# Three kinds of moves at the head of a routed expert stage: first two jobs, segments' and gates' products, register loads, fills

## The reference

```python
h = mod(x_flat[:, :2].sum(axis=1).astype(int32), 8)      # x_flat: layer-normed x
sel = stack([h, mod(h + 1, 8)], axis=1)                  # two neighbouring experts for a token
for e in range(8):
    w = any(sel == e, axis=1) / 2
    out += w[:, None] * (relu(x_flat @ W1[e] + b1[e]) @ W2[e] + b2[e])
x = x + tanh(g_ffn[1]) * out
```

## Time and profile before

| | us |
|---|---|
| median of 3 runs | 358.47 (357.48 to 359.72) |
| the profiled execution | 358.9 |
| its span in the trace | 357.1 |
| TensorE busy | 306.1 (86%) |
| VectorE busy | 195.1 (55%) |
| ScalarE busy | 158.2 (44%) |
| GpSimd busy | 163.3 (46%) |

### The profile page before, as it was taken

The page is one execution under the profiler, slowest core; times in us unless marked ns, Lnnn a source line. Parts: engine busy times, 40 slices in busy tenths (PEclk is TensorE's granted clock), DMA queues, the critical chain, the costliest instruction groups (busy, mean ns, idle before and its releaser), DMA issues.

```text
span 357.1 us, 8461 instructions
## 1 busy us (share of the span) xinstructions
PE 306.1 (86%) x2870; PEld 250.3 (70%) x2882; DVE 195.1 (55%) x592; ACT 158.2 (44%) x335; POOL 163.3 (46%) x345
## 2 busy tenths in 40 slices
PE   8997995978998999977999999986585996969995
PEld 3657652978998999534677777753265996869895
DVE  7558757233433442465788878656713653435563
ACT  1253602111544552433867676872103663435462
POOL 8550403763665534234555464511470045655542
PEclk9999989896999999999999999999568999989999
DMA  7939992284212210446765552089543012222110
GB/s 209 352 87 372 332 259 74 72 187 111 67 58 67 60 39 31 125 106 171 144 157 148 157 129 60 6 270 289 194 90 16 2 32 59 53 45 53 38 31 25
DMA packets 35889, 42.63 MB, mean 119 GB/s; under 512 B 4868, under 2 KB 30511, under 8 KB 34687
## 3 DMA queue, kind: packets, MB, share of 16 engines
q1 hardware_dynamic: 28872, 31.79, 31.2%
q0 software_dynamic: 3664, 8.73, 10.5%
q10 hardware_dynamic: 3312, 1.58, 1.7%
HBM read 30.84 MB, written 10.96 MB: 117 GB/s over the span
## 4 chain that ended last, share of the span: by engine, by line
PE 60%; DVE 14%; another core or an unknown queue 7%; issue 7%; DMA 4%; ACT 3%; POOL 3%; DVEq 1%; SPq 0%; ACTq 0%; POOLq 0%
PE bank L1254 9%; PE pairB L1045 6%; PE pairA L1045 6%; PE bank L1054 5%; PE bank L1723 4%; PE pairB L1244 4%; PE pairA L1693 3%; PE pairA L1244 3%; PE pairB L1709 3%; PE pairB L344 2%; PE pairA L344 2%; DVE maxi L1793 1%; DMA x<-in_x 1%; PE bank L1741 1%
## 5 line engine op out<-in xcount | busy, mean ns | idle before, releaser
L1254 PE MATMUL bank<-wring,prob 128*128 x312 | 44.3, 287 | 11.8 <-DVE prob L1310 6.9
L1254 PEld LDWEIGHTS bank<-wring,prob 128*128 128x128 f32 x312 | 39.6, 199 | 14.1 <-issue 13.6
L1793 DVE TENSOR_REDUCE maxi<-pairA 128x8 f32<-128x1024 f32 x30 | 36.7, 1222 | 14.3 <-PE pairA L1693 12.9
L1765 ACT ACTIVATE prob<-pairB 128x1024 f32<-128x1024 f32 x30 | 30.7, 1024 | 14.5 <-PE pairB L1709 14.4
L1359 POOL DMA_INDIRECT out_x<-qs,inv_i x16 | 15.9, 996 | 45.5 <-DVE qs L1323 44.4
L1155 POOL DMA_INDIRECT back_d<-ysb,inv_i x23 | 22.7, 988 | 28.1 <-DVE ysb L1116 24.9
L1150 POOL DMA_INDIRECT qs<-rows_b_d,inv_i x23 | 22.4, 976 | 23.3 <-DVE inv_i L760 16.7
L300 POOL TENSOR_TENSOR lnv<-lnv,neg_half 128x4 f32<-128x4 f32 (+1 forms) x12 | 14.8, 1232 | 29.5 <-DVE lnv L295 29.5
L1122 DVE COPY xtT<-bank 128x128 f32<-128x128 f32 x23 | 6.7, 292 | 38.0 <-PE bank L1031 27.0
L1281 ACT ACTIVATE xn<-wring 128x516 f32 x37 | 23.4, 633 | 7.9 <-DVE job_i L850 7.4
L1323 DVE SCALAR_TENSOR_TENSOR qs<-bank,job,qs 128x128 f32 x39 | 13.6, 349 | 23.8 <-PE bank L1254 13.5
(11 more groups left out here) (327 smaller groups left out, 703.5 us busy)
## 6 DMA issues: line engine op xcount, KB each, us to landing
wring<-in_wts SPq DMA_DIRECT2D x8, 768.0 KB, 8.3
wring<-in_wts SPq DMA_DIRECT2D x8, 514.0 KB, 5.2
ks<-kparts_d SPq DMA_DIRECT2D x12, 192.0 KB
qs<-qparts_d SPq DMA_DIRECT2D x12, 192.0 KB
kparts_d<-parts SPq DMA_DIRECT2D x8, 192.0 KB, 2.6
qparts_d<-parts SPq DMA_DIRECT2D x8, 192.0 KB, 3.0
ctx_s<-kparts_d SPq DMA_DIRECT2D x6, 192.0 KB
ctxT<-qparts_d SPq DMA_DIRECT2D x6, 192.0 KB
```

The lines of the kernel that those rows point to most:

```text
L1254: j = eng.matmul(bank[1 + i % 2][:, 0:D], act[:, i % 2, c_, :], down_weights(e, o), start=(c_ == 0), stop=(c_ == C1 - 1))
L1765: eng.activation(prob[:, at.half(5), :, :].rearrange("p h t -> p (h t)"), turned_in(at.unit(5))[:, :, :].rearrange("p a t -> p (a t)"), AC ...
L1793: eng.reduce_max(maxi[:, at.half(0), :], scores_in(at.unit(0))[:, :, :].rearrange("p a (h t) -> p (a h) t", t=T), AX).then_inc(s("mx"), 1)
```

## The change

Three things change, all in stage d.

- Fills: WARM[7] (behind the places' product) goes from 3 to 12, WARM[8] (behind the jobs' sums) from 2 to 4, and WARM[9] from 3 to 13. The last group also moves: from behind the gates' products to the head of TensorE's part of the routing, ahead of the wait for the places' tables.
- Order: the segments' transpose with `segT` and the gates' products with the gates' four operations leave `route_d` and become functions (`seg_pe`, `gate_pe`, `seg_dve`, `gate_dve`), which `experts_d` calls. TensorE's order at the head of the stage becomes turn of tile 0, segments' transpose, up(0), gates' products, up(1), turn of tile 1, register loads, down(0), and then up(2) and so on. VectorE's becomes copy of tile 0, `segT`, relu(0), gates, relu(1), copy of tile 1, register load, and then the loop without relu(0) and relu(1).
- Registers: jobs 0 and 1 use the constant tile 0 and the constant experts 0 and 1 on TensorE, so that nothing of theirs waits for `te` or the loads. All eight registers are still loaded. ScalarE's part is unchanged.

```diff
--- before.py
+++ after.py
@@ -76,7 +76,7 @@
 
 
 
-    WARM = (26, 14, 16, 10, 30, 12, 3, 3, 2, 4, 6, 2, 18)
+    WARM = (26, 14, 16, 10, 30, 12, 3, 12, 4, 13, 6, 2, 18)
     A_WARM = 4
     V_WARM, B_WARM = (20,), (4, 1, 2, 8)
     ctx = ExitStack()
@@ -852,14 +852,19 @@
                 eng.reduce_sum(seg[:, :], seg_at[:, :, :], AX).then_inc(s("job_made"), 1)
                 eng.wait_ge(s("job_made"), 2)
                 eng.tensor_copy(b2_i[:, :], seg[:, :]).then_inc(s("b2_i"), 1)
+            DV.append(dve)
+
+            def seg_dve(eng):
                 eng.wait_ge(s("job_sums"), 2)
                 eng.tensor_scalar(segT[:, :], segTp, back, None, ALU.subtract).then_inc(s("job_made"), 1)
+
+            def gate_dve(eng):
+                c = chain(eng, "dve")
                 eng.wait_ge(s("job_sums"), 3)
                 c.link(eng.tensor_tensor(away, of_job, iota_p[:, 0:NJ], ALU.subtract))
                 eng.tensor_scalar(low, away, -1.0, half_gate[:, 0:1], ALU.is_ge, ALU.mult)
                 c.link(eng.tensor_scalar(wrap, away, 0.0, None, ALU.is_le))
                 c.link(eng.tensor_tensor(gate, low, wrap, ALU.mult))
-            DV.append(dve)
 
             def act(eng):
                 eng.wait_ge(s("tile"), 3)
@@ -867,6 +872,7 @@
             AC.append(act)
 
             def pe2(eng):
+                warm(eng, bank[5], WARM[9])
                 eng.wait_ge(s("hotk"), 2)
                 eng.wait_ge(s("hotb"), 2)
                 for b in range(NB):
@@ -880,13 +886,16 @@
                 eng.matmul(at_tile, part[0:TT, :], begun[:, 2, :], start=True, stop=True)
                 eng.matmul(at_back, back, begun[:, 2, :], start=True, stop=True).then_inc(s("job_sums"), 1)
                 warm(eng, bank[5], WARM[8])
+            PE.append(pe2)
+
+            def seg_pe(eng):
                 eng.wait_ge(s("job_made"), 2)
                 eng.transpose(segTp, seg[:, :], ident[:, :]).then_inc(s("job_sums"), 1)
+
+            def gate_pe(eng):
                 eng.wait_ge(s("job_made"), 3)
                 eng.matmul(of_job, segT[:, :], begun[:, 2, :], start=True, stop=True).then_inc(s("job_sums"), 1)
-                warm(eng, bank[5], WARM[9])
-            PE.append(pe2)
-            return gate
+            return gate, (seg_dve, gate_dve), (seg_pe, gate_pe)
 
         def registers(engine, row, n):
 
@@ -1189,7 +1198,9 @@
                     eng.dma_start(x[:, g * GB:(g + 1) * GB, :], v[:, g * GB:(g + 1) * GB, :]).then_inc(s(f"x_in{g}"), 16)
             SP.append(sp_back)
 
-        def experts_d(wts, gate):
+        def experts_d(wts, gate, late_dve, late_pe):
+            seg_dve, gate_dve = late_dve
+            seg_pe, gate_pe = late_pe
 
             n = {k: s(f"{k}_d") for k in ("xTp", "xT", "h", "half", "act", "yp", "y", "ups")}
             UP = 3
@@ -1216,8 +1227,13 @@
                 else:
                     wait(eng, n["ups"], i - 1)
 
+            def tile_of(buf, tau, lo):
+                if isinstance(tau, int):
+                    return buf[:, tau, lo:lo + D]
+                return buf[:, ds(tau, 1), lo:lo + D].rearrange("p a d -> p (a d)")
+
             def down_weights(e, o):
-                return wd[:, ds(e, 1), o:o + D].rearrange("p a d -> p (a d)")
+                return tile_of(wd, e, o)
 
             def job_block(engine, row, k):
                 return registers(engine, job_i[0:1, row, k * BLOCK:(k + 1) * BLOCK], (TT, NE)[row])
@@ -1242,7 +1258,7 @@
                 for f in range(C1):
                     g_, o = divmod(f, C1 // 2)
                     j = eng.matmul(P[:, g_, o * T:(o + 1) * T], w[:, f * 128:(f + 1) * 128],
-                                   xT_all[:, ds(tau, 1), :].rearrange("p a t -> p (a t)"), start=True, stop=True)
+                                   tile_of(xT_all, tau, 0), start=True, stop=True)
                 j.then_inc(n["h"], 1)
 
             def down(eng, i, e):
@@ -1256,19 +1272,25 @@
                 j.then_inc(n["yp"], 1)
 
             def pe(eng):
+
+                turn_over(eng, 0)
+                seg_pe(eng)
+                up(eng, 0, 0)
+                gate_pe(eng)
+                up(eng, 1, 0)
+                turn_over(eng, 1)
                 eng.wait_ge(s("te"), 2)
                 job_tiles = job_block(mybir.EngineType.PE, 0, 0)
-                expert = job_block(mybir.EngineType.PE, 1, 0)
-                turn_over(eng, 0)
-                for i in range(NI):
+                expert = [0, 1] + job_block(mybir.EngineType.PE, 1, 0)[2:]
+                down(eng, 0, expert[0])
+                for i in range(2, NI):
                     up(eng, i, job_tiles[i])
                     if i % BLOCK == BLOCK // 2 and i + BLOCK // 2 < NI:
                         job_tiles += job_block(mybir.EngineType.PE, 0, i // BLOCK + 1)
                         expert += job_block(mybir.EngineType.PE, 1, i // BLOCK + 1)
                     if i % 2 == 0 and i // 2 + 1 < TT:
                         turn_over(eng, i // 2 + 1)
-                    if i >= 1:
-                        down(eng, i - 1, expert[i - 1])
+                    down(eng, i - 1, expert[i - 1])
                 down(eng, NI - 1, expert[NI - 1])
             PE.append(pe)
 
@@ -1328,11 +1350,16 @@
                 eng.tensor_tensor(xs[:, t, D:2 * D], xs[:, t, D:2 * D], b2r[:, t % R, :], ALU.add).then_inc(s("xb2"), 1)
 
             def dve(eng):
-                eng.wait_ge(s("te"), 2)
+                xT(eng, 0)
+                seg_dve(eng)
+                relu_dve(eng, 0)
+                gate_dve(eng)
+                relu_dve(eng, 1)
+                xT(eng, 1)
                 job_tiles = job_block(mybir.EngineType.DVE, 0, 0)
-                xT(eng, 0)
-                for i in range(NI):
-                    relu_dve(eng, i)
+                for i in range(1, NI):
+                    if i > 1:
+                        relu_dve(eng, i)
                     if i % 2 == 0 and i // 2 + 1 < TT:
                         xT(eng, i // 2 + 1)
                     if i >= 1:
@@ -1894,8 +1921,8 @@
             eng.tensor_copy(less_s[:, :], less_f[:, :]).then_inc(s("less"), 1)
             c.link(eng.tensor_tensor(oh[:, :, :], bc(iota_e[:, :], 1, NB), bc(d_, 2, NE), ALU.is_equal))
         DV.append(d_dve)
-        gate_d = route_d()
-        experts_d(A["wts1"], gate_d)
+        gate_d, late_dve, late_pe = route_d()
+        experts_d(A["wts1"], gate_d, late_dve, late_pe)
 
         emit()
```

## The result

In one measurement on one chip the kernel before took 359.7 us (median of 20 runs) and the changed kernel 357.13 (20 runs, 353.16 to 361.8): 0.9939 of the time, 95% interval 0.9914 to 0.9964. That is 0.6% faster and lies within 1%.

What follows compares the result with a forecast made beforehand. It took late TensorE signals beside GpSimd's bias gathers, a hold until 270.67, to decide the case. For the profiled run 358.9 - 3.68 (two jobs) + 0.2 = 355.4; median 355.0, range 352.9 to 357.0.

Steps and rivals of the forecast that it cites:

- Fills: Groups of 13, 12 and 4 at stage d's head lie inside waits, cost nothing and keep the clock at 1.00.
- Order up to up(1): Head of stage d: up(0) starts at 257.65 and takes 1.06; up(1) is done at 260.0 instead of 264.89.
- Register loads: TensorE's loads, moved behind the first jobs, start at 259.0 and take 0.59 each; down(0) starts at 260.8.
- one job only: Rival: TensorE's loads wait for its products, up(2)'s signal is held, gain one job, 1.84 us: median 356.6; chance 0.15.
- the trace disagrees: Against the skill's 200 ns a register (3.2 us for TensorE's sixteen), the trace shows eight loaded in 0.59 us.
- The hold's begin: TensorE's signals come late only from about 263.7, when the bias gathers start; everything up to relu(2) passes.
- The hold's end: Late signals last until 270.67, set by GpSimd's queue of gathers until their data have come, unmoved by the change.
- What stands behind it: After the hold relu(3) follows where relu(1) did: two jobs ahead, 3.68 us, less 0.2 for a pending add_job(1).
- I leave the slow windows as they are: Behind the hold, the slow windows (clock 0.66 from 270 to 275) were taken as unchanged.
- The hold follows TensorE: Rival: hole belongs to the program's place, all 4.9 us kept, 353.6; more than two jobs or all, chance 0.25.
- Given back in later holds: Rival: some 18 us of later unknown waits cost a fifth more, gain gone, 358.5; chance 0.11.
- Slower: Rival: clock falls despite the fills, places' product and gathers move 2.5 us later, median 361.0; chance 0.04.

Runs made afterwards that it cites:

- after: Profiled execution of the changed kernel, unaltered: 359.25 us with a span of 357.4; stage d from its first rank product (L708) to the end 107.18 us.
- nobias_after: Changed kernel without the 16 bias gathers, zeros added instead (second biases left out), on chip A: 344.1 us, stage d 95.40 us.
- after_third: Changed kernel, unaltered, measured again on chip E: 357.5 us, 0.9923 of the kernel before, stage d 106.85 us.
- bias_late: Changed kernel with the first four bias gathers waiting for job 5's upward products, on chip B: 326.22 us, 1.15% faster than the kernel before.
- plain_after_2: Changed kernel without stage d's gathers (plain SyncE row loads, rows unsorted, no second biases; scatters kept), on chip C: stage d 86.03 us.
- spread_after: Changed kernel with the table of bias pairs in 16 copies, eight partitions sharing each, on chip A: 0.9858 of the kernel before, stage d 106.85 us.
- nobias_before: Kernel before without bias gathers (second biases left out), on chip B: 1.0015 of the kernel before, stage d 89.74 us.
- nobias_before_2: Kernel before without bias gathers, repeated on chip D: 335.15 us against 330.59 for the kernel before, stage d 91.19 us.

## Why the prediction was right or wrong

It said 355.0 from 358.47, 3.5 less; measured is 2.6 less (357.13 from 359.7), 0.13 above the range. The 358.47 that the prediction started from is the median of the first three of the 20 runs, and that of all 20 is 1.2 higher; by the ratio the result would be inside (358.47 x 0.9939 = 356.3). That it would lie near the line of 1% was right. Its steps, with 3.06 added to its times:

- **Fills: right.** All three groups lie in waits. The places' product still has 0.32 us of idle time ahead of it and begins at stage time 4.27 (4.26 before); the jobs' sums at 8.39 (8.41 before); GpSimd's first gather at 6.39 (6.41). The clock is 1.00 up to 265.
- **Order up to up(1): right.** up(0) at 260.38 (forecast 260.71), up(1) done at 262.97 (263.06). The two took 1.16, not 1.06, and the gates' products 0.41 (0.4).
- **Register loads: right, with margin.** Trace of after, the line of the loads (duration min/median/max, first and last start):

```profile
L902 PEldq TENSOR_LOAD <-job_i x10: 586/589/597, 260.8 to 331.8; - x10
```

 The first starts at 260.8, 1.3 sooner than my 262.06, and down(0) at 263.20 (263.86). The rival "one job only", by late loads, didn't come about. The Trainium skill ("Runtime: NRT & Kernel Launch", Instruction fetch mechanics) gives some 200 ns a register even in bulk; eight registers in 0.59 us are 74 ns each, here as before. But by its own terms the page speaks of loads from HBM, and these read `job_i`, which lies in the core's SBUF, so the prediction's "the trace disagrees" compared two different loads.
- **The hold's begin: the step that failed.** The prediction read from one lone gather that only bias gathers hold signals, and so let everything up to 263.7 (266.8 in after) pass: relu(0), the gates, relu(1), copy of tile 1, up(2), relu(2). In fact the row gathers hold too. relu(0) comes 0.9 late, the gates 2.0, relu(1) 5.9. Behind relu(1) stands the copy of tile 1 in VectorE's order, and behind that up(2), at 269.87 and at the low clock instead of about 264.8. The prompt answer at 263.08 beside the eighth row gather was taken as proof, and so was that at 305.01. There the row gather beside it had begun only 0.36 us before the products' end at 304.98:

```profile
304.62 0.97 POOL L1349 DMA_INDIRECT qs<-rows_d_d,inv_i  x1 [0.30 <-issue]
```

 In `nobias_after` row gathers alone hold up(1) 3.7 us. What sorts a prompt answer from a late one beside a row gather is not shown.
- **The hold's end: right in its time.** Forecast 273.73, measured 274.00, and 23.5 to 23.8 in stage time in every kernel with the bias gathers at the head. The reason given, "until its data have come", doesn't fit: the last of these gathers' packets end at 271.93 before, behind the 270.67, and at 274.79 in after.
- **What stands behind it: one job, not two.** relu(2) is pending at 274.00 where relu(3) was forecast, which the prediction had named as a sign that it is wrong. The gain at the head is one job (1.84), less 0.3 for the hold's later end, plus 0.9 for a shorter time at the low clock behind it: before, TensorE came back at 271.55 with eight products of 2.07; in after the cold up(2) and down(1) run inside the hold and up(3) takes 1.15 at 273.65. The first four relus behind the held one need 7.3 us, not 8.2. Sum 2.4, and job 10's relu is 2.4 sooner (38.5 against 40.9). "I leave the slow windows as they are" was the second wrong term, in the other direction.
- **The rivals.** "One job only" gave the size (356.6 predicted for it) by a wrong mechanism. "The hold follows TensorE" was half right: relu(1)'s hold did follow, 4.9 us sooner in stage time and just as long, and a second hold at the old place took half of that back. "Given back in later holds" did not happen: from job 10 on the gaps sum to 20.8 us against 22.6, and from its relu to the end it is 68.7 against 69.0 (68.5 in `after_third`). "Slower" did not happen.

So of the 5.0 us by which the products of job 1 come sooner (stage time 12.7 for 17.7), 2.4 reach job 10. Without any hold the change is worth 3.3 to 3.6 us of stage d, by single profiles.

**Open.** Why a chip is of one kind or the other, and whether it stays so; whether the updates are held on TensorE's side or on the way, since the trace has only their arrival; whether GpSimd's issuing or the indirect transfers hold them; why up(0)'s signal is prompt or at most 0.9 late and up(1)'s is the first to be later than that, in every kernel with gathers on such a chip; what the order is worth without the fills; and whether the changed kernel gains its 3.3 us on chips like B, which rests on `bias_late` and the kernels without gathers.

## What to carry to other kernels

A "remote" release with no other core means a signal whose sender is known from the program: set its end beside the waiters' start, and if several such signals arrive in a burst, look for what runs beside them on every engine, and don't take one prompt case as the proof that a neighbour is harmless. Moving work up the path pays only up to the first wait that the move doesn't touch. Look up in every profile when the clock came back before you put a difference of 1 or 2 us down to an edit, and put fills and order to the test together and apart. Where time depends on the chip this much, compare on one chip, and for a step that TensorE's signals pace try products in place of GpSimd's gathers (0.9767 on a chip with late signals, 1.0027 on one without, where it is 5.5 us behind the changed kernel with late bias gathers).

## What the runs showed of the hardware

- TensorE's semaphore updates reached ScalarE and VectorE up to 5.9 us late (up(1)'s, 5.8 before) while GpSimd issued indirect gathers, in bursts, on chips A, C and E and in the first profiles of both kernels; in the eight kernels profiled on B and D no job's was over 0.25 us late. VectorE's and ScalarE's update for down(0) was prompt (0.15 us) beside a held one. With the gathers of stage d gone and its scatters left in, no job's signal was over 0.25 us late on chip C (`plain_after_2`).
- The same one-core kernel took 330.6 us on two chips and 356.8 to 361.3 on three, 8 to 9% apart, each chip used once.
- Four gathers by 128 partitions from eight rows had packets of 4096 bytes with a median of 0.89 us and a maximum of 1.53 (after); with 16 copies of the rows it was 0.18 and 0.39 (`spread_after`).
- The granted clock came back from 0.50 to 1.00 at stage time 14.65 in one profile of a kernel and at 18.05 in another of the same kernel, and stage d was 89.74 and 91.19 us (`nobias_before`, `nobias_before_2`).
